# Two products of the time-mixing layers move from VectorE to GpSimd, and the denominators move ahead of the second scans

## The reference, cut to what matters

```
def step(carry, kv_t):
    p, q, o = carry
    kt, vt = kv_t
    no = jnp.maximum(o, u + kt)
    A = jnp.exp(o - no)
    E = jnp.exp(u + kt - no)
    y = (A * p + E * vt) / (A * q + E)
    no2 = jnp.maximum(w + o, kt)
    A2 = jnp.exp(w + o - no2)
    E2 = jnp.exp(kt - no2)
    return ((A2 * p + E2 * vt, A2 * q + E2, no2), y)
...
x = x + jnp.tanh(g_xattn[0]) * _L0_xattn_ref(8, 256, 512, L0_xattn_w, L0_xattn_u, _layernorm(x, axis=-1), ctx_2048)
...
x = x + jnp.tanh(g_xattn[2]) * _L2_xattn_ref(8, 256, 512, L2_xattn_time_decay, L2_xattn_time_first, _layernorm(x, axis=-1), ctx_2048)
```

## Time and profile before

| | us |
|---|---|
| three runs | 1669.52, 1674.18, 1676.49 |
| median | 1674.18 |
| span of the profiled execution | 1676.2 |
| DVE busy over the span | 1414.7 (84%) |
| PE busy | 1356.3 (81%) |
| POOL busy | 540.3 (32%) |

### The profile page before, as it was taken

How to read it: one execution, slowest core, us unless ns; L and a number is a source line. 1 busy time by engine, 2 the same in 40 slices (tenths; PEclk the granted TensorE clock), 3 DMA queues, 4 the chain that set the end, 5 groups by cost and what they waited for, 6 DMA issues and landing times. The chain is left out here.

```text
span 1676.2 us, 23554 instructions
## 1 busy us (share of the span) xinstructions
PE 1356.3 (81%) x6594; PEld 1015.3 (61%) x6614; DVE 1414.7 (84%) x3035; ACT 951.7 (57%) x2011; POOL 540.3 (32%) x607
## 2 busy tenths in 40 slices
PE   4888548886999777466664893599999999999999
PEld 2444324444788643254532783589887888877777
DVE  6999878984877698799479899889999899997787
ACT  4477746662433152776425441688888888853343
POOL 0000025553110000000006132326776677666552
PEclk9899879997999966688895997799999999999999
DMA  6230020000000040265300010447887987779885
GB/s 223 94 129 13 1 82 1 0 0 1 0 1 0 2 152 1 93 197 175 95 0 1 28 43 0 126 138 226 241 255 226 279 248 250 251 231 266 234 237 171
DMA packets 92659, 197.46 MB, mean 118 GB/s; under 512 B 16104, under 2 KB 25960, under 8 KB 91808
## 3 DMA queue, kind: packets, MB, share of 16 engines
q0 software_dynamic: 26912, 89.94, 18.9%
q1 hardware_dynamic: 65664, 106.61, 18.8%
HBM read 181.04 MB, written 15.47 MB: 117 GB/s over the span
## 5 line engine op out<-in xcount | busy, mean ns | idle before, releaser
L2568 POOL DMA_INDIRECT L3f_gd<-rows,idx x160 | 184.6, 1154 | 169.6 <-DVE L3f_gd L2808 136.7
L2568 POOL DMA_INDIRECT L3f_gu<-in_L_ffn_e_up,idx x160 | 179.3, 1120 | 70.3 <-issue 46.0
L2632 PE MATMUL L3f_o_ps<-L3f_euh,L3f_ath 128*128 128x512 f32 x352 | 143.5, 408 | 15.9 <-DVE L3f_atl L2786 10.6
L2623 PE MATMUL L3f_h_ps<-L3f_xh,L3f_edh 128*128 128x512 f32 (+1 forms) x384 | 145.7, 379 | 0.0
L2623 PE MATMUL L3f_h_ps<-L3f_xl,L3f_edh 128*128 128x512 f32 (+1 forms) x384 | 142.7, 372 | 0.0
L2623 PE MATMUL L3f_h_ps<-L3f_xh,L3f_edl 128*128 128x512 f32 (+1 forms) x384 | 142.7, 372 | 0.0
L2632 PE MATMUL L3f_o_ps<-L3f_euh,L3f_atl 128*128 128x512 f32 x352 | 139.1, 395 | 0.0
L2632 PE MATMUL L3f_o_ps<-L3f_eul,L3f_ath 128*128 128x512 f32 x352 | 138.6, 394 | 0.0
L2608 PE MATMUL L3f_g_ps<-L3f_oh 128*128 128x128 f32 x704 | 100.3, 289 | 44.9 <-DVE L3f_oh L2773 40.3
L2608 PEld LDWEIGHTS L3f_g_ps<-L3f_oh 128*128 128x128 f32 x704 | 95.8, 203 | 53.6 <-issue 49.5
L2822 DVE SCALAR_TENSOR_TENSOR X<-L3f_gu,L3f_coef,X 128x512 f32<-128x512 f32 x160 | 119.7, 748 | 1.0
(11 more groups left out here) (595 smaller groups left out, 3758.5 us busy)
## 6 DMA issues: line engine op xcount, KB each, us to landing
L3f_eu<-in_L_ffn_e_up SPq DMA_DIRECT2D x96, 256.0 KB
L3f_ed<-in_L_ffn_e_down SPq DMA_DIRECT2D x96, 256.0 KB
L2x_ed<-in_L_ffn_e_down SPq DMA_DIRECT2D x32, 256.0 KB, 3.3
rows<-L2x_eo SPq DMA_DIRECT2D x32, 256.0 KB, 2.2
wgu<-in_L_ffn_w_gate_upT SPq DMA_DIRECT2D x4, 1408.0 KB, 8.2
X<-in_x SPq DMA_DIRECT2D x4, 1024.0 KB, 10.4
L0x_V<-in_ctxT SPq DMA_DIRECT2D x8, 512.0 KB, 3.4
L1f_C<-in_ctx SPq DMA_DIRECT2D x2, 2048.0 KB, 13.3
```

Of the source, the lines that this page charges most:

```text
L2568: pool.indirect_dma_start(buf[j % ND][:, :], None, table, bass.IndirectOffsetOnAxis(ap=idx[:, j:j + 1], axis=0)).then_inc(sem[j % ND], 16)
L2623: last = pe.matmul(h_ps[h][:, 0:cols], lhsT=w[h][:, c, :], rhs=x[:, c, 0:cols], start=(c == 0 and m == 0), stop=(c == DC - 1 and m == 2))
L2632: last = pe.matmul(o_ps[a][:, :], lhsT=w[h][:, a * P:(a + 1) * P], rhs=x[h][:, :], start=False, stop=False)
```

## The change

`value` (ev) and `den * r` go to POOL in both phases, and in L0x also `E * V`, the key weight with the bonus times the value (`own_value`). In L0x the sum `den = E + q` is written between the two scans, as it already was in L2x. `y` of L0x is kept in `s` and no longer in `r`, with the waits that follow from it: ACT overwrites `r` once both products that read it are done, and DVE overwrites `s` once PE has turned `y` back. The number of products is the same.

```
-    y = r if first else ph.sb("y", [P, DC, T])
+    y = s if first else ph.sb("y", [P, DC, T])
...
         def invert(b):
             act.wait_ge(den_ready, b + 1)
-            if b and first:
-                act.wait_ge(yT_ready, TB * b)
-            elif b:
+            if b:
                 act.wait_ge(m_ready, b)
+                act.wait_ge(t_ready, b)
...
+        def value(b):
+            pool.wait_ge(ek_ready, b + 1)
+            pool.wait_ge(v_in[b % 3], 16 * (b // 3 + 1))
+            if b:
+                pool.wait_ge(p_ready, b)
+                if not first:
+                    pool.wait_ge(s_ready, b)
+            pool.tensor_tensor(ev[:, :, :], ek[b % 2][:, :, :], V[b % 3][:, :, :], ALU.mult).then_inc(ev_ready, 1)
+
+        def own_value(b):
+            pool.wait_ge(den_ready, b + 1)
+            pool.wait_ge(E_ready, b + 1)
+            pool.tensor_tensor(E[b % 2][:, :, :], E[b % 2][:, :, :], V[b % 3][:, :, :], ALU.mult).then_inc(EV_ready, 1)
+
+        def correct(b):
+            pool.wait_ge(r_ready, b + 1)
+            pool.tensor_tensor(den[:, :, :], den[:, :, :], r[:, :, :], ALU.mult).then_inc(t_ready, 1)
...
+        value(0)
+        for i in range(B):
+            if first:
+                own_value(i)
+                if i + 1 < B:
+                    value(i + 1)
+                correct(i)
+            else:
+                if i:
+                    mean_rows(i - 1)
+                correct(i)
+                if i + 1 < B:
+                    value(i + 1)
...
             last.then_inc(q_ready, 1)
-            if not first:
-                dve.wait_ge(q_ready, b + 1)
-                if b:
-                    dve.wait_ge(y_ready, b)
+            dve.wait_ge(q_ready, b + 1)
+            if b:
+                dve.wait_ge(y_ready, b)
+            if first:
+                dve.wait_ge(E_ready, b + 1)
+                dve.tensor_tensor(den[:, :, :], E[b % 2][:, :, :], q[:, :, :], ALU.add).then_inc(den_ready, 1)
+            else:
...
         def invert(b):
             dve.wait_ge(r_ready, b + 1)
-            dve.tensor_tensor(den[:, :, :], den[:, :, :], r[:, :, :], ALU.mult).then_inc(t_ready, 1)
             dve.wait_ge(s_ready, b + 1)
```

More of the change, by code:

```diff
@@ L592, in _, with mean_rows @@
                     pool.memset(sv[h][j][:, :, :, HD:HD + 1], 1.0).then_inc(filled, 1)
+        def value(b):
[13 more added lines that the diff above has]
+            pool.tensor_tensor(den[:, :, :], den[:, :, :], r[:, :, :], ALU.mult).then_inc(t_ready, 1)
+        def mean_rows(b):
+            pool.wait_ge(x_ready, TB * (b + 1))
+            ts = slice(TB * b, TB * (b + 1))
+            pool.tensor_tensor(stats[:, ts, 1:5:3], rowsum[:, ts].unsqueeze(2).to_broadcast([P, TB, 2]),
+                               part[:, 0:1].unsqueeze(2).to_broadcast([P, TB, 2]), ALU.mult).then_inc(mean_ready, 1)
         if own:
@@ L637, in make_keys, with sums @@
             last.then_inc(kb_ready, 1)
-        def value(b):
+        def sums(b):
             dve.wait_ge(ek_ready, b + 1)
-            dve.wait_ge(v_in[b % 3], 16 * (b // 3 + 1))
-            if b:
[L643 to L647, removed]
             if b:
@@ L670, in ratio @@
             h = b % 2
[L671 to L678, removed]
             dve.wait_ge(p_ready, b + 1)
             dve.wait_ge(p0_ready, b + 1)
-            if b:
+            if b and first:
+                dve.wait_ge(yT_ready, TB * b)
+            elif b:
                 dve.wait_ge(m_ready, b)
@@ L692, in invert @@
             dve.wait_ge(r_ready, b + 1)
-            dve.tensor_tensor(den[:, :, :], den[:, :, :], r[:, :, :], ALU.mult).then_inc(t_ready, 1)
             dve.wait_ge(s_ready, b + 1)
-            if b:
+            if b and not first:
                 dve.wait_ge(yT_ready, TB * b)
@@ L748, in _ @@
         dve.wait_ge(w_ready, 1 if first else 2)
-        value(0)
         if first:
@@ L767, in _ @@
                 context(i, 1)
-            if i + 1 < B:
-                value(i + 1)
             invert(i)
```

## The result

| us | median | lowest to highest | runs | ratio to before, 95% interval |
|---|---|---|---|---|
| before, run beside it | 1671.85 | 1668.13 to 1676.49 | 4 | |
| after | 1696.49 | 1695.02 to 1699.97 | 4 | 1.0164 [1.0144, 1.0185] |

The changed kernel is slower by 24.6 us between the two medians. 1696 was predicted. The spans of the two profiled executions lie 1698.3 - 1676.2 = 22.1 us apart; the sum made for them was +21.7.

The account below looks back on a forecast made before the run. DVE was taken to bound both phases, with a loop through PE and ACT as long in L2x. L0x +2.6 and L2x +19.1 sum to +21.7 us, giving 1696 us on the median's scale, range 1678 to 1708.

Parts of the forecast that it names:

- Turns: Both mixing phases: DVE instructions reading two SBUF tensors, scans included, lose 2.10 us of each 2.30 us POOL product.
- rival A: Scans are not held by POOL: L0x -14, L2x +18 us, 1678, no measurable change; chance 0.15.
- rival B: Both engines stream side by side at this size: L0x -16, L2x -3 us, 1655; chance 0.12.
- rival C: Products take 2.53 us, +7; late ev reaches the next L2x scans, 17.4 us per batch, +9; 1712; chance 0.10.
- L0x: Whole phase +2.6 us: seven batches of 19.44 us +2.1, last batch +1.6, first ev -1.1.
- the first ev: Start of L0x: ev lies beside statistics of rows and saves 1.1 us, or 0 if x is late.
- Make_keys has no POOL product beside it: Mixing phases: make_keys was taken to meet no POOL product, so no hold was charged there.
- L2x: Whole phase +19.1 us: six batches at 15.9 against 13.28 +15.7, batch 0 +2.7, last batch +0.7.
- Batch 0: First L2x batch: three POOL turns, 6.3 us, replace two DVE products and waits, 3.6: +2.7 us.
- The loop from y to r gets a little shorter: L2x batches: PE's 0.43 us wait for xn goes, so the loop falls from 9.74 to 9.3 us.
- The stretch from r to the next scan: L2x batches: two products, two POOL turns of 2.1 us and hand-overs make 6.6 us instead of 3.65.
- One of the signs of being wrong: L2x: r later than 9.7 us behind y would say ACT or PE, not the turns, sets the phase.

Follow-up runs that it names:

- experiment eight: Kernel before with only the changed L0x, L2x left as before: 1674.07 us, ratio to before 1.0025.
- experiment two: Kernel before plus a spare POOL instruction per L2x batch, memset in odd and copy in even batches: 1672.31 us in one run.
- experiment nine: Kernel after, with PE in L2x writing x into y's PSUM tile twice more while it waits for y: 1686.12 us, ratio to before 1.0085.
- experiment four: Kernel after, with ACT in L2x making r before it copies rows and keeps x: 1685.86 us, ratio to before 1.0076.

## Why the prediction was right, point by point

**Turns.** Right, the scans too, which no row had shown: each product costs DVE 4.54 - 2.42 = 2.12 us where it falls on an instruction that is held; 2.10 had been taken. The whole of POOL's product, 2.35 us where it ran unhindered, would have been too much by 0.2 us, as in the earlier trace rows. The scans that were held rule out rival A, and y at 3.35 us beside a product rules out rival B. A product took 2.34 to 2.38 us where nothing held it, not the 2.53 of rival C.

**L0x.** +2.6 predicted. The first instruction behind the phase starts 2.9 us later in the profiled execution:

```profile
197.76 0.18 DVE L837 TENSOR_REDUCE ternary_tot<-ternary_s_ps 128x1 f32<-128x24 f32 x1 [1.14 <-PE ternary_s_ps L818]
```

(before: 194.84), and experiment eight has +3.8 in the medians. The batch was 19.55 for 19.44, and seven of them cost 2.2 us for the 2.1 of the sum. The last one had its two holds (p scans of 6.67 us), but cost 0.6 us for 1.6: the wait for PE's last turning back fell from 2.30 to 1.50 us, which the sum had left as it was. Another term failed the other way: the first ev was to win 1.1 us beside statistics. It ran earlier, beside `make_keys`, and held its second line:

```profile
22.89 2.35 DVE L667 TENSOR_SCALAR L0x_E<-L0x_ek,L0x_u 128x256 f32<-128x256 f32 x4
```

1.14 us before. "Make_keys has no POOL product beside it" was wrong for the first batch, and so was the reading that work with one SBUF input is never held: this instruction reads one tensor and one number per channel. The Trainium skill, in the section named at experiment two (SBUF — State Buffer, "Who interferes with whom"), names tensor_scalar among the operations that can take both ports and contend; the trace agrees, with 1.21 us lost. The statistics and the additions from PSUM stayed free, as predicted. The two misses, 1.0 and 1.2 us, cancel, so that the total of L0x is right in part by luck.

**L2x.** +19.1 predicted, +24.9 measured (start 1.98 us later, end 837.62 for 810.72). Batch 0: ev gone from ahead of q, -1.14, and 16.92 for 13.12 us from q to q, together +2.66, predicted +2.7. The last batch: +1.2 for +0.7. Batches 1 to 6: (817.51 - 716.75) / 6 = 16.79 us by the first and last q scan, for 15.9. So the step that was mis-sized is "The loop from y to r gets a little shorter ... 9.3". PE's wait for xn went as predicted, but I had followed PE's waits and not its clock, which fell in this stretch. The loop was 10.13 us in the batch shown, and 9.95 on average in the six (9.28 to 10.19). With the clock at 1.00, in experiment nine, it is 7.73: the 9.3 holds at neither. 0.65 us in each of six batches is 3.9 of the missing 5.8. The stretch from r to the next scan (6.77 for 6.6), with the 0.08 us from the start of a scan to the end of the y ahead of it, which the sum left out, is 1.5, and the last batch 0.5. Rival C's 17.4 us per batch is nearer to 16.79 than 15.9, but not by its mechanism: in these batches no ev reached into the next scans.

One of the signs of being wrong came true, r later than 9.7 us behind y, "which would say that ACT or PE, and not the turns, sets L2x". The rows show both. Along the chain of a batch the stretch from r to the next scan, where the turns are, grew by 3.1 us, from 3.70 on average to 6.77; the loop, by the same six batches, only by 0.5, from 9.49 to 9.95. DVE has the time to wait for that loop because its own products are gone, and 2.0 to 2.1 us of a batch come back when r is taken off the loop (experiment four) or PE is kept busy (nine).

**The sum.** Up to the end of L2x the profiled execution lost 26.9 us: 2.9 in L0x and 24.9 in L2x, less 0.9 between them. Behind it, where nothing was changed, it was 4.8 us shorter than that of before: 860.7 us from the first instruction behind L2x to the end of the span, where that of before took 865.5. In the traces of the nine experiments, with the same code there, this part takes 857.8 to 862.2 us, so that it was the profiled execution of before that ran long. It is none of the four runs of before: the times on record lie 1.7 us above their spans, which would make it about 1677.9. The agreement of 21.7 with 22.1 is thus partly luck: the medians differ by 24.6. And 1696 was met so closely because the median of three to which 21.7 was added, 1674.18, lies 2.3 above the median of four.

**What it would take.** Of a batch's +3.5 us in L2x some 1.4 to 1.5 stay as holds when nothing waits for r (experiments nine and four), and some 2.0 to 2.1 are there because r waits for the loop through PE and ACT. In L0x three products save 3.63 us and cost two holds of 2.1; the one that lies in the cover costs nothing, and alone it makes the kernel faster.

## What to carry to other kernels

A product moved from VectorE to GpSimd is worth its VectorE time only while VectorE does work that isn't held: look in the timeline for a stretch as long as GpSimd's instruction (here 2.35 us against 1.14 saved) of additions from PSUM or statistics, and make GpSimd wait for the instruction ahead of that stretch. Outside it each move costs about a microsecond. Where two engines pass work round a loop, look at TensorE's granted clock in the stretch as well as at its waits: the loop ran at 0.77 to 0.82 here, and filling TensorE's pauses with spare matmuls won 10 us.

## What the runs showed of the hardware

- A GpSimd memset of 128x1024 (0.95 us) beside a VectorE instruction with two SBUF inputs costs it nothing; a copy (1.04 us) costs 0.86, a product 1.73 to 2.12.
- A GpSimd product of 128x1024 takes 2.34 us from two tiles, and 1.89 with the same tile as both inputs.
- A VectorE tensor_scalar with a single tensor input is held as well (2.35 for 1.14 us).
- Matmuls added to TensorE's idle time made the kernel faster by 10 us, with a granted clock of 1.00 for 0.77 to 0.82. How the pauses and the clock belong together is open: experiment four had shorter pauses ahead of the turn back (2.12 us for 5.29) and a lower clock (0.73).
